# The second latent pass by pairs of items on two halves of TensorE's rows, the fourth attention's small banks rearranged, and weight rounding moved beside the tile attention

## The chip, the cores and the metric

One core of one Trainium2 chip runs the whole program in one launch. The metric is the device time of one execution in microseconds (us). The kernel before took 1465.81 us, the median of three runs (1461.55 to 1468.51).

## The reference, cut to what matters

The program is four layers over an activation `x` of 32 items by 128 rows by 128 columns in float32; each layer adds an attention and a feed-forward block to `x`. What the change touches is the routed block of layer 1, the ternary weights of layer 2, and the latent attention of layer 3:

```python
# layer 1, ffn: 63 rows of each batch picked, attention over them (16 heads), then gelu MLP, scattered back
# layer 2, ffn: weight_quant(w) = clip(round(w * scale), -1, 1) / scale, scale = 1 / mean(|w|)
# layer 3, ffn, attention half (N_HEADS 16, HEAD_DIM 8, KV_LATENT 64):
q = (x @ Wq.T).reshape(b, t, N_HEADS, HEAD_DIM)
latent = layernorm(x @ Wdkv.T, ln_g, ln_b)          # 64 wide
k = (latent @ Wuk.T).reshape(...); v = (latent @ Wuv.T).reshape(...)
q = apply_rope(q); k = apply_rope(k)
scores = jnp.where(causal, einsum('bhqd,bhkd->bhqk', q, k) / sqrt(HEAD_DIM), -inf)
out = einsum('bhqk,bhkd->bhqd', softmax(scores), v) @ Wo.T
```

In words: for every one of the 32 items, a 128 x 64 latent is normalised over its 64 columns, scaled by `ln_g` and shifted by `ln_b`, and multiplied with a 64 x 384 weight (key, key with halves turned for the rotation, value).

## The kernel before, in words

`x_all` holds the 32 items in SBUF for the whole run. The program is a list of stages (`phases`); all five engines meet at a barrier after each (`phase_end`, L971). Inside a stage every engine walks a software pipeline written with `steps` or `whole_steps`: at step t the stage function with lag n works on item t - n. What an engine waits for is a counting semaphore.

**The latent stage** (`latent_*`, from L1612) has two passes. The first turns x, multiplies it with `w_h1` (320 columns), rotates the queries and keeps the raw latents in `lat_raw`. Then VectorE works out mean and scale of all 32 latents at once. The second pass, over 32 items, is for each item:

- ScalarE `scale` (L1704) writes the normalised latent, 128 rows by 64 columns, to `o_sb`; two slots.
- TensorE `turn_latent` (L1737) transposes it into bank 4 or 5 of PSUM.
- ScalarE `take_turned` (L1711) applies `ln_g` and `ln_b` per partition and writes `oT`, 64 partitions by 128; two slots.
- TensorE `keys` (L1743) multiplies it with `w_h2` (64 x 384) into bank 6 or 7. A float32 product is two MATMUL instructions in the trace.
- VectorE `key` (L1661, L1662) multiplies the two 128-column halves with the rotation table into `probs`; GpSimd `key` (L1679) adds them into `kv_all`; ScalarE `take_v` (L1716) copies the value.

**The attentions** L0 to L4 share four functions. One step of `attention_tensor` is: `halves(.., 0)` (half of the raw scores of item t-2 and of the final scores of item t-4, L671, L696, L703, L713), `turns` (all small transposes and products), `mask_whole` (L722), `halves(.., 1)`, `weighted` (L860, item t-5), `mask_strips`. `turns` has a first part (transposes of o, q and k into bank 6, L800, L807, L808) and a last part (the product of oT with the output weight, L783, the transposed maxima, L776, and the picking of p times v, L827, in bank 7). `LOW` names the attentions whose last part comes first: there the turned maxima lie in bank 6, the output product in bank 7, the last part runs ahead of the first, VectorE takes o and adds the product to the stream ahead of taking qT, kT and oT, and `weighted` waits for the addition three items back in place of the copied maxima. Before, `LOW` holds L0, L2 and L3; L4, the causal latent attention with 16 heads over 32 items, is not in it.

**The rounding** of layer 2's weights (`expand_aside`) runs on GpSimd in the stage that expands the routed rows (`expand_*`), after the clearing of `v_wide`. The stage before it is the attention L1 over four tiles, in which GpSimd has little to do.

Of the kernel before, what the change touches and what calls it, by code (L numbers as in the profile page):

```python
# [11 lines left out]
ALU = mybir.AluOpType  # L12
# [3 lines left out]
B, S, D = 32, 128, 128  # L16
# [8 lines left out]
RING = 4  # L25
# [98 lines left out]
def build(nc, t_in, out):  # L124
    with ExitStack() as ctx_:
# [9 lines left out]
        def after(name, n=0):  # L135

            return sem(name), n + begun.get(name, 0)

        def sb(name, shape, dt=F32):
            return ctx_.enter_context(nc.sbuf_tensor(name, shape, dt))  # L140
# [130 lines left out]

        TURN_LAG = {True: 8, False: 6}

        LOW = ("L0", "L2") + ("L3",)

        def turned_max(L):

# [668 lines left out]
        causal = sb("causal", [128, 4, 128], BF16)  # L946
        rope = sb("rope", [128, 4, 128])
        w_h1 = sb("w_h1", [128, 320])
        w_h2 = sb("w_h2", [64, 384])
        w_o3 = sb("w_o3", [128, 128])  # L950
        gate_w = sb("gate_w", [128, N_EXP3])
        gate_b = sb("gate_b", [128, N_EXP3])
# [659 lines left out]
        lat_raw = ctx_all[:, 0:8, :].rearrange("p a b -> p (a b)").rearrange("p (b n) -> p b n", b=B)  # L1612
        lat_stat = ctx_all[:, 8, 0:6 * B].rearrange("p (b n) -> p b n", b=B)
        lat_scale, lat_shift = ctx_all[:, 9, 0:B], ctx_all[:, 9, B:2 * B]
        turned_halves = probs[:, 0, 0:1024].rearrange("p (k n) -> p k n", k=RING)

        def latent_vector(dve):
            V = nc.vector
            inv_both = inv_all[:, 0:B]
            V.scalar_tensor_tensor(shift_all[:], mean_all[:], -1.0, inv_ln[:], ALU.mult, ALU.mult  # L1620
                                   ).then_inc(sem("la_shift"), 1)

            def query(b, k):
                dve.wait_ge(*after("used", b + 1))
                wait_reuse(dve, after("la_q"), b, RING)
                src, own = ps[:, 2 + k, :], inv_both[:, b:b + 1]
                half = turned_halves[:, k, :]
                V.scalar_tensor_tensor(half[:, 0:128], src[:, 0:128], own, rope[:, 0, :], ALU.mult, ALU.mult)
                V.scalar_tensor_tensor(half[:, 128:256], src[:, 128:256], own, rope[:, 1, :], ALU.mult, ALU.mult)  # L1629
                V.bn_stats(lat_stat[:, b, :], src[:, 256:320]).then_inc(sem("la_halves"), 1)  # L1630
            steps(dve, B, [(3, query)])


            dve.wait_ge(sem("la_halves"), B)
            c = moments_taken["v"] = moments_taken.get("v", 0) + 1
            q = Seq(dve, sem("vector_step"), moments_taken)
            part, var, root, twice, apart = (moment[:, i, 0:B] for i in range(5))
            st = lat_stat
            q.count(V.tensor_tensor(apart, st[:, :, 1], st[:, :, 4], ALU.subtract))
            q.count(V.tensor_tensor(part, st[:, :, 2], st[:, :, 5], ALU.add))  # L1640
            q(V.tensor_tensor(twice, st[:, :, 1], st[:, :, 4], ALU.add))
            q.count(V.scalar_tensor_tensor(apart, apart, 0.25, apart, ALU.mult, ALU.mult))
            q(V.tensor_tensor(var, inv_both, inv_both, ALU.mult))
            q(V.scalar_tensor_tensor(part, part, 1.0 / LATENT, apart, ALU.mult, ALU.add))
            q(V.tensor_tensor(var, var, part, ALU.mult))
            q(V.tensor_scalar(var, var, 1e-5, None, ALU.add))
            dve.sem_inc(sem("variance"), 1)
            dve.wait_ge(sem("deviation"), c)
            q(V.reciprocal(apart, root))
            q(V.scalar_tensor_tensor(part, apart, -0.5, apart, ALU.mult, ALU.mult))  # L1650
            q(V.tensor_tensor(part, part, var, ALU.mult))
            q(V.scalar_tensor_tensor(apart, part, 1.5, apart, ALU.add, ALU.mult))
            q(V.tensor_tensor(lat_scale, apart, inv_both, ALU.mult))
            q(V.scalar_tensor_tensor(lat_shift, twice, -0.5, lat_scale, ALU.mult, ALU.mult))
            dve.sem_inc(sem("la_scaled"), 1)

            def key(b, k):
                dve.wait_ge(sem("la_kv"), b + 1)
                wait_reuse(dve, after("la_k"), b, RING)
                half, src = turned_halves[:, k, :], ps[:, 6 + k % 2, :]  # L1660
                V.tensor_tensor(half[:, 0:128], src[:, 0:128], rope[:, 2, :], ALU.mult)  # L1661
                V.tensor_tensor(half[:, 128:256], src[:, 128:256], rope[:, 3, :], ALU.mult  # L1662
                                ).then_inc(sem("la_key_halves"), 1)
            dve.wait_ge(sem("la_q"), B)
            steps(dve, B, [(3, key)])

        def latent_gpsimd(pool):
            pads_gpsimd(pool, 16)
# [4 lines left out]
                nc.gpsimd.tensor_tensor(q_all[:, b, :], half[:, 0:128], half[:, 128:256],  # L1673
                                        ALU.add).then_inc(sem("la_q"), 1)

            def key(b, k):
                pool.wait_ge(sem("la_key_halves"), b + 1)
                half = turned_halves[:, k, :]
                nc.gpsimd.tensor_tensor(kv_all[:, b, 0:128], half[:, 0:128], half[:, 128:256],  # L1679
                                        ALU.add).then_inc(sem("la_k"), 1)  # L1680
            steps(pool, B, [(4, query)])
            steps(pool, B, [(4, key)])

        def latent_scalar(act):
            nc.scalar.activation(w_h1[:], w_h1[:], ACT.Copy, scale=col("norm1")).then_inc(sem("la_weights"), 1)
# [13 lines left out]
            act.wait_ge(sem("la_scaled"), 1)  # L1699
            act.wait_ge(sem("la_raw"), B)  # L1700

            def scale(b, k):
                wait_reuse(act, after("la_latent_turned"), b, 2)
                nc.scalar.activation(o_sb[:, k % 2, 0:LATENT], lat_raw[:, b, :], ACT.Identity,  # L1704
                                     bias=lat_shift[:, b:b + 1], scale=lat_scale[:, b:b + 1]
                                     ).then_inc(sem("la_latent"), 1)

            def take_turned(b, k):
                act.wait_ge(sem("la_latent_turned"), b + 1)
                wait_reuse(act, after("la_kv"), b, 2)  # L1710
                nc.scalar.activation(oT[0:LATENT, k % 2, :], ps[0:LATENT, 4 + k % 2, 0:128], ACT.Identity,  # L1711
                                     bias=col("ln_b", LATENT), scale=col("ln_g", LATENT)).then_inc(sem("la_latentT"), 1)

            def take_v(b, k):
                act.wait_ge(sem("la_key_halves"), b + 1)
                nc.scalar.activation(kv_all[:, b, 128:256], ps[:, 6 + k % 2, 256:384],  # L1716
                                     ACT.Copy).then_inc(sem("la_v"), 1)
            steps(act, B, [(0, scale), (1, take_turned), (3, take_v)])

        def latent_tensor(pe):  # L1720
            pe.wait_ge(sem("la_weights"), 1)
# [9 lines left out]
            steps(pe, B, [(1, turn_x(pe)), (2, queries)])  # L1731
            pe.wait_ge(sem("la_raw"), B)

            def turn_latent(b, k):
                pe.wait_ge(sem("la_latent"), b + 1)
                wait_reuse(pe, after("la_latentT"), b, 2)
                nc.tensor.transpose(ps[0:LATENT, 4 + k % 2, 0:128], o_sb[:, k % 2, 0:LATENT],  # L1737
                                    ident[:]).then_inc(sem("la_latent_turned"), 1)

            def keys(b, k):  # L1740
                pe.wait_ge(sem("la_latentT"), b + 1)
                wait_reuse(pe, after("la_v"), b, 2)
                nc.tensor.matmul(ps[:, 6 + k % 2, 0:384], oT[0:LATENT, k % 2, :], w_h2[:], start=True,  # L1743
                                 stop=True).then_inc(sem("la_kv"), 1)
            steps(pe, B, [(1, turn_latent), (2, keys)])

# [132 lines left out]
        def expert_tensor(pe):  # L1881
# [39 lines left out]
            def group(i, k):  # L1921
# [64 lines left out]
            (w_tgt[:, 0:128], t_in["W_tgtT"]), (w_tgt[:, 128:256], t_in["W_outT"][0:128, :]),  # L1986
            (w_out2[:], t_in["W_outT"][128:256, :]),
            (w_h1[:, 0:128], t_in["WqT"]), (w_h1[:, 128:256], t_in["WqT_turned"]), (w_h1[:, 256:320], t_in["WdkvT"]),
            (w_h2[:, 0:128], t_in["WukT"]), (w_h2[:, 128:256], t_in["WukT_turned"]), (w_h2[:, 256:384], t_in["WuvT"]),
            (w_o3[:], t_in["WoT"]), (gate_w[:], t_in["gateT"]), (gate_b[:], t_in["gate_b"].partition_broadcast(128)),  # L1990
            (b1_col[:], t_in["b1T"]), (b2_col[:], t_in["b2T"]),
            (bias_cols[:, 0:1], t_in["b_in"].rearrange("(c p) -> p c", p=128)),
# [4 lines left out]
            (col("L2_b"), t_in["L2_b"].partition_broadcast(128)),  # L1997
            (col("router_b"), t_in["router_b"].partition_broadcast(128)),
            (rw_row[:], t_in["router_w"].rearrange("d one -> (one d)").partition_broadcast(128)),
        ] + [(col(n, t_in[n].shape[0]), t_in[n].rearrange("(s one) -> s one", one=1))  # L2000
             for n in ("g_res", "ln1", "ln2", "norm1", "norm2", "ln_g", "ln_b")]

# [117 lines left out]

        def expand_aside(pool):
            q = Seq(pool, sem("aside_seq"), moments_taken)
            V = nc.gpsimd
            pads_gpsimd(pool, 8)
            for w, i in ((w1_nat, 0), (w2_nat, 1)):
                q(V.tensor_scalar(w, w, inv_w[:, i:i + 1], MAGIC, ALU.mult, ALU.add))
                q(V.tensor_scalar(w, w, MAGIC, -1.0, ALU.subtract, ALU.max))
# [38 lines left out]
        def row_counts(**more):  # L2168
# [16 lines left out]
            dict(vector=gather_vector, scalar=gather_scalar, tensor=gather_tensor),  # L2185
            dict(vector=lambda e: attention_vector(e, "L1", TILES, 16, False, True),
                 counts=attention_counts("L1", TILES, 16, True),
                 gpsimd=lambda e: attention_gpsimd(e, "L1", TILES, 16, False),
                 scalar=lambda e: attention_scalar(e, "L1", TILES, 16, False, True),
                 tensor=lambda e: attention_tensor(e, "L1", TILES, 16, 3, tile_mask, w_o1[:])),  # L2190
            dict(vector=expand_vector, scalar=expand_scalar, tensor=expand_tensor, gpsimd=expand_aside),
            dict(vector=lambda e: attention_vector(e, "L2", B, 8, True, False),
                 counts=attention_counts("L2", B, 8, False),
                 gpsimd=lambda e: attention_gpsimd(e, "L2", B, 8, True),
# [149 lines left out]
```

## Time and profile before

| what | value |
|---|---|
| median of three runs | 1465.81 us |
| the profiled execution, whole | 1465.44 us |
| its span | 1463.7 us |
| TensorE's mean granted clock | 0.911 of full speed |
| TensorE busy | 1306.9 us, 89% of the span |
| latent stage, second pass | 923.6 to 987.0 us |
| attention L4 | 987.1 to 1191.6 us |

A time in a row is counted from the start of the span. PE is TensorE's MATMUL, PEld its weight load, DVE is VectorE, ACT ScalarE, POOL GpSimd; PEq, ACTq and so on are their sequencers. The column PEclk is the clock granted to TensorE, 1.00 being 2.4 GHz and 0.50 being 1.2 GHz. A shape such as 64*128 behind a matmul is the rows and columns of the array that it uses.

### The profile page before, as it was taken

What the parts mean: (1) busy time and instruction counts of PE and PEld (TensorE: products, weight loads), DVE (VectorE), ACT (ScalarE), POOL (GpSimd) and SP (SyncE); (2) the same over time, 40 slices, a digit from 0 to 9 for tenths busy, and PEclk for the clock granted to TensorE, in tenths of its full rate; (3) what the DMA queues carried; (4) which work ended last, traced back from release to release, by engine and by line L of the source; (5) the groups of instructions that cost most, each with busy time, mean ns of one, the idle gap of its engine ahead of it and who ended that gap; (6) DMA issues with size and microseconds to landing.
All of it is one profiled execution on the core that took longest, in us unless ns stands there. A gap on an engine that the chain in (4) does not pass through costs nothing. (4 is left out here: it accounts for less than half of the span.)

```text
span 1463.7 us, 37014 instructions
## 1 busy us (share of the span) xinstructions
PE 1306.9 (89%) x13899; PEld 861.5 (59%) x13899; DVE 932.4 (64%) x2810; ACT 605.9 (41%) x1375; POOL 277.2 (19%) x782
## 2 busy tenths in 40 slices
PE   3999988839759979998999997899999969999998
PEld 2888876635447754444657885337888844444443
DVE  4677749975367858996336886325777744454554
ACT  2788845641326642222443556542444421111111
POOL 0122211310313320000002223222454520000000
PEclk9999998958869989997998998656999979999999
DMA  9400000000000000000000000001000000000000
GB/s 288 121 3 3 3 2 2 2 1 1 2 1 2 3 2 1 1 1 1 1 1 2 3 3 1 1 0 59 3 3 3 3 2 0 15 8 7 7 7 15
DMA packets 26390, 21.31 MB, mean 15 GB/s; under 512 B 5936, under 2 KB 22512, under 8 KB 26224
## 3 DMA queue, kind: packets, MB, share of 16 engines
q1 hardware_dynamic: 25216, 18.87, 4.6%
q8 instruction: 112, 1.84, 0.5%
q14 instruction: 54, 0.44, 0.1%
q10 hardware_dynamic: 1008, 0.16, 0.1%
HBM read 16.93 MB, written 2.10 MB: 13 GB/s over the span
## 5 line engine op out<-in xcount | busy, mean ns | idle before, releaser
L703 PE MATMUL ps<-kT,qTm 32*128 32x128 f32 x3200 | 250.9, 291 | 1.2 <-issue 0.6
L671 PE MATMUL ps<-qTm,kT 32*128 32x512 f32 (+1 forms) x1024 | 249.1, 550 | 1.8 <-ACT probs L574 1.4
L703 PEld LDWEIGHTS ps<-kT,qTm 32*128 32x128 f32 x3200 | 226.1, 202 | 6.9 <-issue 4.2
L1933 PE MATMUL ps<-kv_all,ctx_all 128*128 128x512 f32 x256 | 134.1, 605 | 5.8 <-DVE kv_all L1846 5.8
L1870 ACT ACTIVATE kv_all<-ps,b_col 128x512 f32<-128x512 f32 x64 | 44.0, 687 | 216.5 <-PE ps L1911 216.5
L1911 PE MATMUL ps<-q_all,ctx_all 128*128 128x512 f32 x256 | 132.4, 600 | 0.0
L380 DVE TENSOR_REDUCE neg_max<-ps 128x8 f32<-128x1024 f32 x72 | 87.7, 1219 | 67.6 <-PE ps L703 67.3
L574 ACT ACTIVATE probs<-ps 128x1024 f32<-128x1024 f32 x72 | 73.8, 1024 | 119.7 <-PE ps L713 119.7
L860 PE MATMUL ps<-probs,v_wide 128*32 128x128 f32 x3200 | 115.2, 277 | 8.5 <-DVE o_sb L429 3.7
L1846 DVE TENSOR_SCALAR kv_all<-ps,b_col 128x512 f32<-128x512 f32 x64 | 48.0, 750 | 116.4 <-PE ps L1911 116.4
L671 PEld LDWEIGHTS ps<-qTm,kT 32*128 32x128 f32 x1024 | 85.2, 189 | 47.9 <-issue 38.8
L499 POOL CAST nm<-neg_max 128x16 bf16<-128x16 f32 (+1 forms) x132 | 27.0, 204 | 426.2 <-DVE neg_max L367 158.2
L375 DVE TENSOR_REDUCE neg_max<-ps 128x4 f32<-128x512 f32 x128 | 82.1, 683 | 34.2 <-PE ps L703 34.1
L394 DVE TENSOR_TENSOR qTm<-ps,hmask 128x512 f32<-128x512 f32 (+1 forms) x132 | 73.4, 556 | 38.4 <-ACT nmT L552 19.7
L570 ACT ACTIVATE probs<-ps,bias_col 128x512 f32<-128x512 f32 x128 | 81.1, 684 | 36.2 <-PE ps L713 36.2
L713 PE MATMUL ps<-nmT,sel_max 32*128 32x128 bf16 x1600 | 95.6, 218 | 0.0
L860 PEld LDWEIGHTS ps<-probs,v_wide 128*32 128x32 f32 x3200 | 80.7, 109 | 24.3 <-issue 13.9
L1529 PE MATMUL ps<-tap_w,xqT 128*128 128x512 f32 x192 | 93.6, 624 | 0.0
L1911 PEld LDWEIGHTS ps<-q_all,ctx_all 128*128 128x128 f32 x256 | 49.1, 192 | 61.3 <-issue 61.3
L564 ACT ACTIVATE probs<-ps,bias_col 128x1024 f32<-128x1024 f32 x64 | 71.4, 1115 | 32.1 <-PE ps L713 32.1
L827 PE MATMUL ps<-pv_pick,pv 128*128 128x72 f32 (+1 forms) x528 | 82.6, 279 | 1.0 <-ACT pv L580 0.9
L580 ACT ACTIVATE pv<-ps 128x256 f32<-128x256 f32 x132 | 50.7, 384 | 72.1 <-PE ps L860 69.6
(379 smaller groups left out, 2703.8 us busy)
## 6 DMA issues: line engine op xcount, KB each, us to landing
ctx_all<-in_ctx SPq DMA_DIRECT2D x4, 1024.0 KB, 10.5
x_all<-in_x SPq DMA_DIRECT2D x4, 512.0 KB, 7.1
out<-x_all SPq DMA_DIRECT2D x8, 256.0 KB, 2.3
ctx_all<-in_W1T SPq DMA_DIRECT2D x1, 1024.0 KB, 5.5
tap_w<-in_conv_wT SPq DMA_DIRECT2D x1, 768.0 KB, 6.9
w_l<-in_w SPq DMA_DIRECT2D x2, 256.0 KB, 3.7
above<-in_c_above SPq DMA_DIRECT2D x1, 256.0 KB, 3.4
rope<-in_c_rope SPq DMA_DIRECT2D x1, 256.0 KB, 2.7
```

The source lines that it names most:

```text
L375: nc.vector.tensor_reduce(neg_max[:, k, per * g:per * g + per], ps[:, raw_bank(L, b, g), 0:N].rearrange("p (h k) -> p h k", h=per), AX.X, ...
L380: nc.vector.tensor_reduce(neg_max[:, k, H2 * u:H2 * u + H2].rearrange("p (a h) -> p a h", a=2), ps[:, 4 * u:4 * u + 2, 0:N].rearrange("p a ...
L570: nc.scalar.activation(probs[:, k % 2, N * g:N * (g + 1)], ps[:, final_bank(L, b, g), 0:N], ACT.Exp, bias=bias).then_inc(sem("probs_ready" ...
L574: nc.scalar.activation(probs[:, k % 2, 2 * N * u:2 * N * (u + 1)].rearrange("p (a n) -> p a n", a=2), ps[:, 2:4, 0:N], ACT.Exp, bias=bias) ...
L671: nc.tensor.matmul(ps[:, bank, at:at + N], kT[rows_of(g), k, :], qTm[rows_of(g), k, 0:N], start=True, stop=False, skip_group_check=True)
L703: last = nc.tensor.matmul(dst, qTm[rows_of(g), k, 128 * i:128 * i + 128], kT[rows_of(g), k, :], start=False, stop=True, skip_group_check=True)
L713: last = nc.tensor.matmul(dst, sel_max[rows_of(g), i, :], nmT[rows_of(g), k, :], start=False, stop=True, skip_group_check=True)
L827: last = nc.tensor.matmul(ps[:, 7, 256 + W * half:256 + W * half + W], pv[:, k % 2, 128 * half:128 * half + 128], pv_pick[:, 0 if heads == ...
L860: last = nc.tensor.matmul(ps[32 * j:32 * j + 32, 7, 128 * half:128 * half + 128], v_tile(k % 2, heads, 4 * half + j, i), probs[:, k % 2, 1 ...
L1529: last = nc.tensor.matmul(dst, xqT[:, k % 2, tap:tap + 128], tap_w[:, tap, :], start=False, stop=tap == 2)
L1911: nc.tensor.matmul(ps[:, c % 2, :], w_up[:, c, :], xm_T[:, k, :], start=True, stop=True).then_inc(sem("mo_hidden"), 1)
L1933: nc.tensor.matmul(ps[:, 4 + e % 2, :], w_down[:, c, :], hid[:, c % 4, :], start=c % 4 == 0, stop=c % 4 == 3).then_inc(sem("mo_down"), 1)
```

## The change

Three things. First, the second latent pass works on 16 pairs of items. The two latents of a pair stand side by side in `o_sb` (128 columns), one transpose turns both, so that item 2p lies on partitions 0 to 63 and item 2p+1 on 64 to 127; `w_h2`, `ln_g` and `ln_b` are loaded a second time on partitions 64 to 127; the two products of a pair use rows 0 to 63 and 64 to 127 of TensorE and two banks; three pairs of banks take turns. VectorE rotates a pair with one instruction, GpSimd adds a pair with one, ScalarE scales with two, and takes the turned latents and the values with one each. Second, L4 joins `LOW`. Third, GpSimd rounds the weights at the end of its part in L1 (`round_weights`), and only clears `v_wide` in the expand stage.

```diff
-        LOW = ("L0", "L2") + ("L3",)
+        LOW = ("L0", "L2") + ("L3", "L4")
-        w_h2 = sb("w_h2", [64, 384])
+        w_h2 = sb("w_h2", [128, 384])
+        pair_halves = probs[:, 0, :].rearrange("p (k i n) -> p k i n", k=RING, i=2)
+        PAIRS = B // 2
+        def pair_banks(p):
+            at = 2 + 2 * (p % 3)
+            return ps[:, at:at + 2, :]
# VectorE
-                V.tensor_tensor(half[:, 0:128], src[:, 0:128], rope[:, 2, :], ALU.mult)
-                V.tensor_tensor(half[:, 128:256], src[:, 128:256], rope[:, 3, :], ALU.mult
+                wide = rope[:, 2:4, :].rearrange("p r n -> p (r n)").unsqueeze(1).broadcast_to([128, 2, 256])
+                V.tensor_tensor(pair_halves[:, k, :, :], pair_banks(p)[:, :, 0:256], wide, ALU.mult
# GpSimd
+                nc.gpsimd.tensor_tensor(kv_all[:, 2 * p:2 * p + 2, 0:128], half[:, :, 0:128], half[:, :, 128:256],
# ScalarE
+            def scale(p, k):
+                wait_reuse(act, after("la_latent_turned"), p, 2)
+                for b in (2 * p, 2 * p + 1):
+                    at = LATENT * (b % 2)
+                    nc.scalar.activation(o_sb[:, k % 2, at:at + LATENT], lat_raw[:, b, :], ACT.Identity,
+                                         bias=lat_shift[:, b:b + 1], scale=lat_scale[:, b:b + 1]
+            def take_turned(p, k):
+                act.wait_ge(sem("la_latent_turned"), p + 1)
+                wait_reuse(act, after("la_kv"), p, 2, 2)
+                nc.scalar.activation(oT[:, k % 2, :], ps[:, k % 2, 0:128], ACT.Identity,
+            def take_v(p, k):
+                act.wait_ge(sem("la_key_halves"), p + 1)
+                nc.scalar.activation(kv_all[:, 2 * p:2 * p + 2, 128:256], pair_banks(p)[:, :, 256:384],
+            steps(act, PAIRS, [(0, scale), (1, take_turned), (3, take_v)])
# TensorE
+            def turn_latents(p, k):
+                pe.wait_ge(sem("la_latent"), 2 * p + 2)
+                wait_reuse(pe, after("la_latentT"), p, 2)
+                nc.tensor.transpose(ps[:, k % 2, 0:128], o_sb[:, k % 2, :], ident[:])
+            def keys(p, k):
+                pe.wait_ge(sem("la_latentT"), p + 1)
+                wait_reuse(pe, after("la_v"), p, 3)
+                for i in range(2):
+                    rows = slice(LATENT * i, LATENT * i + LATENT)
+                    nc.tensor.matmul(pair_banks(p)[:, i, 0:384], oT[rows, k % 2, :], w_h2[rows, :], start=True,
+                                     stop=True).then_inc(sem("la_kv"), 1)
+            steps(pe, PAIRS, [(1, turn_latents), (2, keys)])
# loads: 6 DMAs of w_h2 in place of 3, and 2 more for ln_g, ln_b on partitions 64 to 127
# rounding
-        def expand_aside(pool):
+        def round_weights(pool):
-            pads_gpsimd(pool, 8)
-                 gpsimd=lambda e: attention_gpsimd(e, "L1", TILES, 16, False),
+                 gpsimd=lambda e: (attention_gpsimd(e, "L1", TILES, 16, False), round_weights(e)),
-            dict(vector=expand_vector, scalar=expand_scalar, tensor=expand_tensor, gpsimd=expand_aside),
+            dict(vector=expand_vector, scalar=expand_scalar, tensor=expand_tensor, gpsimd=lambda e: pads_gpsimd(e, 8)),
```

## Rows read from the trace of the kernel before

**Rows 1.** The page's first part: busy time, share of the span, instructions.
```profile
PE 1306.9 (89%) x13899; PEld 861.5 (59%) x13899; DVE 932.4 (64%) x2810; ACT 605.9 (41%) x1375; POOL 277.2 (19%) x782
```
**Rows 2.** Busy time by stretch (length, each engine, PEclk, DMA share, GB/s).
```profile
899.00:902.00 3.00, 3.00 (x15) 1.95 (x14) 2.61 (x13) 2.62 (x12) 1.82 (x4) 0.98 0.00 0
903.00:917.00 14.00, 14.00 (x65) 9.21 (x63) 14.00 (x65) 14.00 (x65) 9.69 (x22) 1.00 0.01 3
917.00:924.00 7.00, 2.17 (x9) 1.03 (x7) 5.86 (x28) 3.69 (x17) 2.49 (x6) 0.93 0.00 0
927.00:984.00 57.00, 57.00 (x90) 18.92 (x90) 14.57 (x60) 27.73 (x88) 13.61 (x30) 0.50 0.00 1
987.00:1012.00 25.00, 23.69 (x233) 16.92 (x237) 12.47 (x17) 5.05 (x8) 4.37 (x11) 0.51 0.27 85
1041.00:1098.00 57.00, 55.47 (x1136) 45.67 (x1134) 42.48 (x90) 27.00 (x40) 28.11 (x50) 1.00 0.01 3
```
**Rows 3.** The chain that ended last, in order of time: start, us, what.
```profile
927.16 1.58 PE ps L1743 x2
928.74 0.35 PE ps L1737
```
**Rows 4.** Instructions in order of time, second pass: ScalarE (start, us, what, [idle before]).
```profile
923.64 0.77 ACT L1704 ACTIVATE o_sb<-ctx_all 128x64 f32<-128x64 f32 x2 [1.61 <-DVEq L1655]
...
946.47 0.45 ACT L1711 ACTIVATE oT<-ps,cols 64x128 f32<-64x128 f32 x1 [0.98 <-PE ps L1737]
946.82 0.26 ACT L1716 ACTIVATE kv_all<-ps 128x128 f32<-128x128 f32 x1
946.98 0.43 ACT L1704 ACTIVATE o_sb<-ctx_all 128x64 f32<-128x64 f32 x1
```
**Rows 5.** The same view, end of the second pass and start of L4.
```profile
986.50 0.45 POOL L1679 TENSOR_TENSOR kv_all<-probs 128x128 f32<-128x128 f32 x1 [0.83 <-DVE probs L1662]
...
987.07 0.47 PE L807 MATMUL ps<-ident,q_all 128*128 128x128 f32 x1 [1.18 <-POOLq L971]
```
**Rows 6.** Single lines: op, count, duration ns min/median/max, first and last start, forms.
```profile
L394 DVE TENSOR_TENSOR qTm<-ps,hmask x132: 405/678/693, 23.2 to 1165.1; 128x512 f32<-128x512 f32 x68, 128x256 f32<-128x256 f32 x64
L580 ACT ACTIVATE pv<-ps x132: 377/384/386, 48.1 to 1186.9; 128x256 f32<-128x256 f32 x132
```
**Rows 7.** L1's final scores: the single line, then in order of time.
```profile
L675 PE MATMUL ps<-qTm,kT x32: 587/640/692, 351.5 to 380.3; 32*128 32x512 f32 x32
...
375.83 1.13 PE L675 MATMUL ps<-qTm,kT 32*128 32x512 f32 x4
```
**Rows 8.** Instructions in order of time, one step of L4.
```profile
1099.86 0.70 PE L671 MATMUL ps<-qTm,kT 32*128 32x512 f32 x2
...
1101.24 1.23 DVE L380 TENSOR_REDUCE neg_max<-ps 128x8 f32<-128x1024 f32 x1 [1.34 <-PE ps L703]
...
1102.38 0.68 DVE L394 TENSOR_TENSOR qTm<-ps,hmask 128x512 f32<-128x512 f32 x1
...
1102.51 0.28 ACT L552 ACTIVATE nmT<-ps 128x128 bf16<-128x128 bf16 x1 [0.16 <-PE ps L827]
...
1103.38 0.24 DVE L423 RECIPROCAL inv_den<-ps 128x16 f32<-128x16 f32 x1
...
1104.17 0.29 DVE L264 BATCH_NORM_STATS2 stats_all<-ctx_all 128x6 f32<-128x128 f32 x1
...
1105.55 0.70 PE L671 MATMUL ps<-qTm,kT 32*128 32x512 f32 x2
```
**Rows 9.** Instructions in order of time, the expand stage's GpSimd and one VectorE.
```profile
390.52 1.19 POOL L2140 MEMSET v_wide<- 128x1312 f32 x1 [15.94 <-SPq L971]
...
392.03 0.70 POOL L2128 TENSOR_SCALAR k_pad<-k_pad,inv_w 128x512 f32<-128x512 f32 x1
...
392.90 0.54 DVE L240 TENSOR_TENSOR moment<-moment 128x4 f32<-128x4 f32 x1
...
401.31 3.97 POOL L2133 TENSOR_TENSOR tap_w<-k_pad,tap_w 128x512 f32<-128x512 f32 x3
```

More of the change, by code:

```diff
@@ L1655, in latent_vector, with key @@
             dve.sem_inc(sem("la_scaled"), 1)
[L1657 to L1660, printed above, removed]
-                V.tensor_tensor(half[:, 0:128], src[:, 0:128], rope[:, 2, :], ALU.mult)
-                V.tensor_tensor(half[:, 128:256], src[:, 128:256], rope[:, 3, :], ALU.mult
+            def key(p, k):
+                dve.wait_ge(sem("la_kv"), 2 * p + 2)
+                wait_reuse(dve, after("la_k"), p, RING)
+                wide = rope[:, 2:4, :].rearrange("p r n -> p (r n)").unsqueeze(1).broadcast_to([128, 2, 256])
+                V.tensor_tensor(pair_halves[:, k, :, :], pair_banks(p)[:, :, 0:256], wide, ALU.mult
                                 ).then_inc(sem("la_key_halves"), 1)
             dve.wait_ge(sem("la_q"), B)
-            steps(dve, B, [(3, key)])
+            steps(dve, PAIRS, [(3, key)])
         def latent_gpsimd(pool):
@@ L1674, in query, with key @@
                                         ALU.add).then_inc(sem("la_q"), 1)
[L1676 to L1679, printed above, removed]
+            def key(p, k):
+                pool.wait_ge(sem("la_key_halves"), p + 1)
+                half = pair_halves[:, k, :, :]
+                nc.gpsimd.tensor_tensor(kv_all[:, 2 * p:2 * p + 2, 0:128], half[:, :, 0:128], half[:, :, 128:256],
                                         ALU.add).then_inc(sem("la_k"), 1)
             steps(pool, B, [(4, query)])
-            steps(pool, B, [(4, key)])
+            steps(pool, PAIRS, [(4, key)])
         def latent_scalar(act):
@@ L1700, in latent_scalar @@
             act.wait_ge(sem("la_raw"), B)
[L1702 to L1716, printed above, removed]
+            def scale(p, k):
[4 more added lines that the diff above has]
+                                         bias=lat_shift[:, b:b + 1], scale=lat_scale[:, b:b + 1]
+                                         ).then_inc(sem("la_latent"), 1)
+            def take_turned(p, k):
+                act.wait_ge(sem("la_latent_turned"), p + 1)
+                wait_reuse(act, after("la_kv"), p, 2, 2)
+                nc.scalar.activation(oT[:, k % 2, :], ps[:, k % 2, 0:128], ACT.Identity,
+                                     bias=col("ln_b"), scale=col("ln_g")).then_inc(sem("la_latentT"), 1)
+            def take_v(p, k):
+                act.wait_ge(sem("la_key_halves"), p + 1)
+                nc.scalar.activation(kv_all[:, 2 * p:2 * p + 2, 128:256], pair_banks(p)[:, :, 256:384],
                                      ACT.Copy).then_inc(sem("la_v"), 1)
-            steps(act, B, [(0, scale), (1, take_turned), (3, take_v)])
+            steps(act, PAIRS, [(0, scale), (1, take_turned), (3, take_v)])
         def latent_tensor(pe):
@@ L1732, in latent_tensor @@
             pe.wait_ge(sem("la_raw"), B)
[L1734 to L1745, printed above, removed]
+            def turn_latents(p, k):
+                pe.wait_ge(sem("la_latent"), 2 * p + 2)
+                wait_reuse(pe, after("la_latentT"), p, 2)
+                nc.tensor.transpose(ps[:, k % 2, 0:128], o_sb[:, k % 2, :], ident[:]).then_inc(sem("la_latent_turned"), 1)
+            def keys(p, k):
[6 more added lines that the diff above has]
+            steps(pe, PAIRS, [(1, turn_latents), (2, keys)])
         GROUPS = B // 4
@@ L1988, in build @@
             (w_h1[:, 0:128], t_in["WqT"]), (w_h1[:, 128:256], t_in["WqT_turned"]), (w_h1[:, 256:320], t_in["WdkvT"]),
-            (w_h2[:, 0:128], t_in["WukT"]), (w_h2[:, 128:256], t_in["WukT_turned"]), (w_h2[:, 256:384], t_in["WuvT"]),
             (w_o3[:], t_in["WoT"]), (gate_w[:], t_in["gateT"]), (gate_b[:], t_in["gate_b"].partition_broadcast(128)),
@@ L1999, in build @@
             (rw_row[:], t_in["router_w"].rearrange("d one -> (one d)").partition_broadcast(128)),
+        ] + [(w_h2[64 * i:64 * i + 64, 128 * c:128 * c + 128], t_in[w])
+             for i in range(2) for c, w in enumerate(("WukT", "WukT_turned", "WuvT"))
+        ] + [(col(n)[64:128, :], t_in[n].rearrange("(s one) -> s one", one=1)) for n in ("ln_g", "ln_b")
         ] + [(col(n, t_in[n].shape[0]), t_in[n].rearrange("(s one) -> s one", one=1))
```

## The prediction

> **What bounds the kernel now.** I read the page's first part, then busy time by stretch, then the chain of waits, then single steps in order of time. TensorE is busy for 89% of the span [rows 1], so the question for each part of the change is whether it shortens TensorE's own work where that is the chain.
>
> In the second latent pass it is. From 927 to 984 us TensorE is busy for 57.00 of 57.00 us at a granted clock of 0.50 (1.2 GHz), while VectorE has 14.57, ScalarE 27.73 and GpSimd 13.61 us of work [rows 2]. The chain is nothing but TensorE: 1.58 us for the key product's two instructions, 0.35 us for the transpose, so 1.93 us an item [rows 3]. The stretches around show that the clock is no property of the stage: it was 1.00 in the first pass (products on 128*128), fell in the gap of 917 to 924 us, in which TensorE did 2.17 us, and stayed low [rows 2]. The instructions that ran at 0.50 use 64 of the 128 rows, or 64 of the 128 columns.
>
> In L4 the middle stretch has TensorE busy for 55.47 of 57.00 us at 1.00, VectorE 42.48 [rows 2]. There it is the engine that counts, and an edit that only reorders it can win nothing but waits.
>
> **Part one, the pass by pairs.** Per pair the change removes one transpose, and puts the two key products on different rows.
>
> Do the two products run at once? No row shows it for 64 rows; the nearest is L1's final score: products on two groups of 32 rows, 512 columns. One instruction takes 587 to 692 ns, yet all four take 1.13 us [rows 7]: that is two after each other, not four. The instructions are the same kind (float32, own banks), so I take full overlap. Bounds for the four key instructions of a pair, from 1.58 us for two [rows 3]: 1.58 (both at once) and 3.16 (one after another). I take 1.58.
>
> The Trainium skill (TensorEngine Tiling (Array Packing), Key Properties) says that changing the tiling mode, not just the tile, drains TensorE. By that rule the drain between the 128-row transpose and the 64-row products stays, but comes 16 times and not 32; no row here prices it alone. It is inside the 0.35 and 1.58 us, and the sum goes by those.
>
> The transpose now loads 128 columns and not 64. The nearest full transpose at the low clock took 0.47 us [rows 5]; I add 0.05 to the 0.35 (bounds 0 and 0.12). So a pair costs 0.40 + 1.58 = 1.98 us at 1.2 GHz, against 3.86 before. Over the pass: from the scaling's start at 923.64 to GpSimd's end at 986.95 it took 63.3 us [rows 4, 5]. After: the first product starts 2.0 us in (two scalings, a transpose, a copy, one scaling more than now), then 16 x 1.98 less the transpose that the last step lacks = 31.3, and a tail: VectorE on 512 columns 0.68 [rows 6], GpSimd on 256, and hand-overs, 1.7 together. That is 35.0, a gain of 28.3 us if the clock stays at 0.50.
>
> The others have room beside 1.98 us. ScalarE: two scalings at 0.34 spacing, the turned latents at 0.35, the values at 0.16 [rows 4] plus 0.12 for the doubled width (0.38 for 256 columns [rows 6] against 0.26 for 128 [rows 4]): 1.32 us a pair. VectorE 0.68. GpSimd: 0.45 at 128 columns [rows 5], 3.97 for three of 512 [rows 9], so about 0.75.
>
> Will the clock stay low? In the pass now half of the array stands idle at any time; with both halves in use nothing does but the gaps. At 896 to 902 us work on the whole array brought the clock from 0.50 to 0.98 within a few us [rows 2]; in L4, on 32-row products, it took until 1012 [rows 2]. The pairs lie between. I give a rise during the pass 62 in 100, after some 10 us of it. Then TensorE would need half of 1.98, 1.0 us a pair, and ScalarE's 1.32 becomes the bound; I take 1.35. With about four pairs at 1.98 and twelve at 1.35: 12 x 0.63 = 7.6 less, of which a later rise takes some: 6.5. Part one gains 28.3 + 6.5 = 34.8 us.
>
> Behind the pass comes L4, whose first 25 us ran at 0.51 [rows 2]. Between the last key product and L4's first transpose then stand VectorE's 0.68, GpSimd's 0.75 and the barrier, about 3 us with TensorE idle; the gap at 917 to 924 dropped the clock. So I expect L4 to start low as before: 0, bounds -10 (it starts high) and +2 (the rise comes later by chance).
>
> **Part two, L4's small banks.** No instruction is added or removed. TensorE's step, 5.69 us from one L671 to the same one a step later (1099.86 to 1105.55 [rows 8]), stays. What moves is VectorE: qTm (1102.38 now) comes behind o, its addition and its statistics, which take 1103.38 to 1104.46 together, 1.1 us [rows 8]. It starts when L380 ends at 1102.47 at best: o, addition and statistics to 1103.5, qTm (0.68) to 1104.2, kT's copy of a quarter of its width to 1104.4. Its new wait, for the copy of the maxima (ends at 1102.79 [rows 8]), is met by then; behind it in VectorE's queue stand kT, oT and the second maxima, and for qTm the next step's scores wait, at 1105.55 [rows 8]. Slack 1.1 us: cost 0. `weighted` waits for an addition that ends 1 us earlier than o does now: it saves 0 to 0.1 us where that was tight. In the drain the product and L827 wait together for the copied p times v, and the addition three items back stands ahead of `weighted`: 0.2 to 0.5 us in each of three last steps. I take +0.5, bounds -2 and +3.
>
> **Part three, the rounding.** GpSimd is idle for 15.94 us before 390.52; the rounding lasts from 392.03 to 405.28, 13.3 us [rows 9]. It would run from 374.6 to 387.9 and end 2.6 us ahead of the stage. In the expand stage it hid behind TensorE's and ScalarE's chain, so its leaving saves only what it cost VectorE there: L240 took 0.54 us on 4 columns beside it [rows 9]; I take -0.4, bounds -0.54 and 0. In L1's tail it meets VectorE's chain of short instructions: 0 to +3. I take +0.2, net -0.2.
>
> The Trainium skill (SBUF — State Buffer, Who interferes with whom) says that a VectorE instruction with two SBUF inputs and a GpSimd instruction that reads SBUF exclude each other for a whole instruction. L240's row agrees. By that rule L448 (two SBUF inputs, three in a row) could be held in L1's tail; the +3 above covers it.
>
> **The loads.** Five more small DMAs on SP's queue, issued in L0, whose loads nobody on the chain awaits: 0.
>
> **Sum**, against the profiled execution's own 1465.44 us (its span 1463.7, and 0.4 under the median, so the same scale): 1465.4 - 34.8 + 0 + 0.5 - 0.2 = 1430.9; I say 1431.
>
> **The rivals.**
> - The clock stays at 0.50 through the pass. For it: 57 us at 0.50 with TensorE busy throughout [rows 2]; against: half of the array was unused. 1465.4 - 28.3 + 0.3 = 1437.4. Chance 25 in 100.
> - The clock is high and L4 starts high too: for it, the pass ends only 3 us before; against, the gap of 917 to 924. L4's first 25 us at 0.51 lose up to 10: 1421 to 1425. Chance 9.
> - The two products don't overlap (the change doesn't do what it says). For it: no row with 64 rows; against [rows 7]. 3.16 + 0.40 = 3.56 a pair, 57 us in all, gain 4.8 us: 1461. Chance 7.
> - Slower: L4's scores wait for qTm. Place: VectorE's new order, with its wait on ScalarE's copy of the maxima. If that copy falls behind ScalarE's second exponential, to where the next step begins now (1105.55 [rows 8]), qTm and kT end 0.9 and the hand-overs 0.3 later, and each of 32 steps grows by 1.2 us: +38. It decides from 1.05 us a step, where it eats part one; time then 1469 to 1475. Against it: the copy stands ahead of that exponential in ScalarE's order. Chance 4.
> The forecast itself has 53; 2 are left for what I don't see.
>
> **How the numbers follow.** The likeliest's own range is 1426 to 1436 (clock rise early or late, drain). The range 1422 to 1442 takes in the rival with the low clock and most of that with L4 high: about 85 in 100 on paper, which I count as 8 in 10. A measurement of this kernel tells about 0.5%, 7.3 us. Faster by more than that: the forecast, the low clock and the high L4, 53 + 25 + 9, and part of the unseen, 0.88; within: no overlap, 0.08; slower 0.04.
>
> **What would show it.** L1743's 64 instructions: starts in twos a few ns apart, a pair's step 1.98 us or, with a clock of 1.00 in the pass, near 1.35 and bounded by ScalarE (right); 3.5 us (no overlap). L4's step 5.69 us with no wait for L394 before L671 and L703 (right). GpSimd's rounding over by 388, and expand as long as before within 0.5 us. The prediction is wrong if the pass takes over 40 us, or if L4's middle step isn't 5.69.

## The result, and the profile after

The changed kernel takes 1422.44 us (median of 4, 1420.91 to 1427.89) against 1466.18 us on the same chip: ratio 0.9712, 95% interval 0.9676 to 0.9748. The medians differ by 43.7 us; 34.5 was said (1430.9 against 1465.4). The median stands 0.4 us inside the low end of the range of 1422 to 1442, and two of its four executions (1420.91 and 1421.04) lie below it. Its profiled execution took 1421.04 us, with a span of 1419.3 us and a mean granted clock of 0.929 (0.911 before).

The page's first part, after:

```profile
PE 1262.0 (89%) x13883; PEld 845.8 (60%) x13883; DVE 930.2 (66%) x2762; ACT 594.9 (42%) x1343; POOL 273.6 (19%) x766
```

The 16 fewer MATMULs are the transposes; TensorE's share is still 89% [rows 1]. Busy time by stretch, after (columns as in [rows 2]):

```profile
923.60:926.90 3.30, 2.86 (x8) 1.06 (x8) 0.19 (x1) 2.92 (x9) 0.00 (x0) 0.50 0.00 0
926.90:930.00 3.10, 3.10 (x10) 1.19 (x9) 1.19 (x2) 2.48 (x8) 1.33 (x2) 0.50 0.00 0
930.00:943.00 13.00, 12.79 (x55) 4.61 (x53) 7.27 (x11) 12.54 (x41) 7.36 (x11) 0.99 0.00 1
...
946.80:951.00 4.20, 2.62 (x38) 1.64 (x38) 1.56 (x3) 1.63 (x3) 0.57 (x1) 0.98 0.50 155
951.00:972.00 21.00, 20.35 (x215) 15.37 (x211) 11.27 (x15) 3.69 (x6) 4.99 (x11) 0.50 0.23 71
1000.00:1057.00 57.00, 56.79 (x1204) 46.04 (x1200) 45.03 (x95) 27.83 (x42) 28.14 (x51) 1.00 0.01 3
```

The second latent pass starts at the low clock, as before, but leaves it at 930.5, after three pairs; from there ScalarE is the full engine (12.54 of 13.00 us). L4 begins high (its first transpose is at 947.6) and the clock falls at 951. From the first scaling at 923.00 to GpSimd's end at 947.37 the pass took 24.4 us, where it took 63.3. In the middle of L4 57 us hold 1204 MATMULs where they held 1136 [rows 2]: L4's step became shorter, 5.45 us and not 5.69, which had been ruled out. The chain of waits in the pass (start, us, what):

```profile
924.96 1.60 PE ps L1753 x4
926.56 0.41 PE ps L1746
926.97 1.58 PE ps L1753 x4
928.55 0.41 PE ps L1746
...
930.76 0.84 PE ps L1753 x4
931.61 0.26 PE ps L1746
```

All four instructions of a pair take the 1.58 us that two took [rows 3], the transpose 0.41. L4, from its transposed maxima to the next step's scores, in order of time:

```profile
1053.54 0.22 PE L776 MATMUL ps<-identb,nm 128*128 128x128 bf16 x1
1053.69 0.41 PE L722 MATMUL ps<-causal,identb 32*32 32x512 bf16 x8
...
1054.02 0.29 DVE L429 TENSOR_TENSOR o_sb<-ps,inv_den 128x128 f32<-128x128 f32 x1
...
1054.75 0.67 DVE L394 TENSOR_TENSOR qTm<-ps,hmask 128x512 f32<-128x512 f32 x1
1054.99 0.39 PE L713 MATMUL ps<-nmT,sel_max 32*128 32x128 bf16 x8
1055.31 1.08 PE L860 MATMUL ps<-probs,v_wide 128*32 128x128 f32 x32
...
1056.65 0.70 PE L671 MATMUL ps<-qTm,kT 32*128 32x512 f32 x2
```

The weighted product (L860) starts 0.32 us after L713 does. The same place in the kernel before (in order of time, not among the rows ahead of the prediction):

```profile
1103.66 0.29 DVE L429 TENSOR_TENSOR o_sb<-ps,inv_den 128x128 f32<-128x128 f32 x1
1103.70 0.39 PE L713 MATMUL ps<-nmT,sel_max 32*128 32x128 bf16 x8
...
1104.20 0.32 PE L860 MATMUL ps<-probs,v_wide 128*32 128x128 f32 x4
```

There it is 0.50 us, and o ends at 1103.95, 0.25 before L860 starts: L860 waited for o. In L1's tail of the changed kernel (in order of time) VectorE is held:

```profile
384.62 3.96 POOL L2144 TENSOR_TENSOR tap_w<-k_pad,tap_w 128x512 f32<-128x512 f32 x3
385.42 3.31 DVE L448 SCALAR_TENSOR_TENSOR x_all<-q_all,place_keep,x_all 128x128 f32<-128x128 f32 x3
388.65 0.28 DVE L414 COPY oT<-ps 128x128 f32<-128x128 f32 x1
389.86 0.86 DVE L448 SCALAR_TENSOR_TENSOR x_all<-q_all,place_keep,x_all 128x128 f32<-128x128 f32 x3
```

### The profile page after: what moved, and what is told of

It reads as the page before. It is cut to its first block and busy times, and to the rows that moved or that the text cites. A ratio compares the mean times of both kernels' runs of the same rounds, so it can differ in the third digit from the quotient of the medians.

```text
span 1419.3 us, 36830 instructions
## 1 busy us (share of the span) xinstructions
PE 1262.0 (89%) x13883; PEld 845.8 (60%) x13883; DVE 930.2 (66%) x2762; ACT 594.9 (42%) x1343; POOL 273.6 (19%) x766
## 5 line engine op out<-in xcount | busy, mean ns | idle before, releaser
L671 PE MATMUL ps<-qTm,kT 32*128 32x512 f32 (+1 forms) x1024 | 251.5, 555 | 2.3 <-ACT probs L574 2.1
L860 PE MATMUL ps<-probs,v_wide 128*32 128x128 f32 x3200 | 116.9, 280 | 4.6 <-DVE o_sb L429 1.7
L671 PEld LDWEIGHTS ps<-qTm,kT 32*128 32x128 f32 x1024 | 85.7, 190 | 48.5 <-issue 39.4
L713 PE MATMUL ps<-nmT,sel_max 32*128 32x128 bf16 x1600 | 96.7, 219 | 0.0
L860 PEld LDWEIGHTS ps<-probs,v_wide 128*32 128x32 f32 x3200 | 81.1, 111 | 19.7 <-issue 6.5
```

The lines of the kernel that those rows point to most:

```text
L671: nc.tensor.matmul(ps[:, bank, at:at + N], kT[rows_of(g), k, :], qTm[rows_of(g), k, 0:N], start=True, stop=False, skip_group_check=True)
L713: last = nc.tensor.matmul(dst, sel_max[rows_of(g), i, :], nmT[rows_of(g), k, :], start=False, stop=True, skip_group_check=True)
L860: last = nc.tensor.matmul(ps[32 * j:32 * j + 32, 7, 128 * half:128 * half + 128], v_tile(k % 2, heads, 4 * half + j, i), probs[:, k % 2, 1 ...
```

## The experiments

**The parts alone.** Three kernels with one part each. A ratio is that of a run's time to the time of the kernel before, measured beside it on the same chip, with its 95% interval; the us behind it are that ratio's gain on the kernel before.

```diff
# a_only: the changed kernel with parts two and three taken back
# b_only: the kernel before with
+        LOW = ("L0", "L2") + ("L3", "L4")
# c_only: the kernel before with round_weights behind GpSimd's part in L1
```

> The kernel before with part one alone (the pass by pairs, and the loads that it needs). Theory after the traces: the pass gains 38.9 us (63.3 to 24.4), and L4's steady step is 5.69 us as before, so 1427 +- 2 us. The prediction's own term was a gain of 34.8: 1431. Rival: that part of the gain belongs to the change of L4 or of the rounding (the clock rises only in their company): the pass then takes over 30 us here.

Measured: 1427.35 us, ratio 0.9737 (0.9717 to 0.9756): 38.6 us. In its trace a pair again takes 1.99 us at first (1.58 and 0.41), then 1.1 and from the eighth on 1.27; the pass is 25.1 us long. The pass's gain is its own.

> The kernel before with L4 in LOW, and nothing else. Theory after the traces: L4's steady step falls from 5.69 to 5.45 us by this edit alone, some 27 steps, so 1459 to 1461 (5 to 6.5 us faster). The prediction's term: step 5.69, 1466. Rival: the shorter step comes from what part one leaves behind (places of the keys, the clock); the step then stays 5.69 here.

Measured: 1460.45 us, ratio 0.9959 (0.9943 to 0.9975): 6.0 us. L4's steps, one after the other:

```profile
1101.52 0.70 PE L671 MATMUL ps<-qTm,kT 32*128 32x512 f32 x2
...
1105.30 0.39 PE L713 MATMUL ps<-nmT,sel_max 32*128 32x128 bf16 x8
1105.62 1.08 PE L860 MATMUL ps<-probs,v_wide 128*32 128x128 f32 x32
...
1106.97 0.70 PE L671 MATMUL ps<-qTm,kT 32*128 32x512 f32 x2
```

5.45 us. From L4's first transpose of q to its last there are 171.0 us (177.2 before), while the drain behind it is 0.6 us longer, as forecast.

> The kernel before with the rounding moved into L1's stage, and nothing else. Theory after the traces: three L448 instructions of VectorE are held beside GpSimd's products of two SBUF inputs (3.3 us in place of 0.86), L1's tail grows by 1.5 to 2 us, the expand stage gains 0.4 to 1.0: 1466 to 1467. The prediction's term: 1465.2. Rival: L1's tail was later in the changed kernel for another reason; L448 x3 then stays near 0.9 us and the stage pair 85.5 us.

Measured: 1466.76 us, ratio 1.0003 (0.9988 to 1.0018): no change in time. The three L448 take 3.32 us, where the changed kernel has 3.31, and from the end of the last copy of v to the next stage's memset there are 17.5 us, where GpSimd's idle time shows 15.94 [rows 9]. The 1.6 us lost in L1's tail are seen in the trace; whether anything gives them back isn't shown. The parts add up to 38.6 + 6.0 - 0.4 = 44.2 us by their ratios, and all three together have 42.2 by theirs (36.9 to 47.5): nothing shows that one part needs another.

**Why L4's step is shorter.** VectorE's order alone:

```diff
-                if L in LOW:
+                if L in LOW or L == "L4":
                     at(6, take_o)
...
-                if L not in LOW:
+                if L not in LOW and L != "L4":
                     at(6, take_o)
```

> The kernel before, in L4 alone VectorE takes o ahead of qT, kT and oT; TensorE's order, the banks and all waits stay as before. Theory: of the 0.24 us a step, 0.185 was the wait of the weighted product (L860) for o, which ended 0.22 us before it started; so here L860 starts right behind L713 and the step is 5.50 us, 5 us in all: 1461. Rival 1: the wait is not for o but for ScalarE's nmT or pv, which this edit leaves: step 5.69. Rival 2: the gain is all in TensorE's own order (L783, L827 first): step 5.69 here and 5.45 in the kernel with L4 in LOW.

Measured: 1461.32 us, ratio 0.9953 (0.9939 to 0.9967). In order of time (its lines from L672 on are one further down):

```profile
1101.03 0.70 PE L672 MATMUL ps<-qTm,kT 32*128 32x512 f32 x2
...
1101.47 0.29 DVE L429 TENSOR_TENSOR o_sb<-ps,inv_den 128x128 f32<-128x128 f32 x1
...
1101.99 0.39 PE L714 MATMUL ps<-nmT,sel_max 32*128 32x128 bf16 x8
...
1102.31 1.08 PE L861 MATMUL ps<-probs,v_wide 128*32 128x128 f32 x32
```

L861 stands 0.32 us behind L714, and the L672 of the next step comes at 1106.53, so a step is 5.50 us. Rival 1 is refuted: ScalarE's copies were left as they were. By time this kernel and `b_only` can't be told apart (the intervals overlap); the split that follows is read from the steps of the traces. Of the 0.24 us, 0.19 was the wait for o, and moving one VectorE instruction removes it. The other 0.05 belongs to TensorE's order: from L783 to L722 there are 1.26 us with the picking product last and 1.20 with the transposed maxima last.

**What the two halves at once are worth.** In one kernel the second product waits for the first:

```diff
                 for i in range(2):
+                    if i:
+                        pe.wait_ge(sem("la_kv"), 2 * p + 1)
                     rows = slice(LATENT * i, LATENT * i + LATENT)
```

> The changed kernel, but the second key product of a pair waits for the end of the first: the same instructions on the same two row halves, not at once. Theory: being at once is what brings the gain, twice: it halves the product's 3.16 us, and with both halves of the array at work the clock rises. Then a pair takes 3.6 us here, the clock stays at 0.50 for most of the pass, the pass takes 58 to 60 us, and the whole 1456 to 1459. Rival 1: the clock rises all the same after some pairs (it asks only for TensorE being busy): some 1.95 us a pair from there, pass 35 to 40 us, 1433 to 1438. Rival 2: the gain was in fewer transposes and hand-overs: 1425.

Measured: 1457.97 us, ratio 0.9927 (0.9909 to 0.9945); the pass took 60.1 us. Busy time by stretch, then the chain:

```profile
927.00:980.00 53.00, 52.13 (x75) 16.74 (x74) 9.91 (x15) 18.14 (x52) 10.15 (x14) 0.50 0.00 0
```

```profile
928.62 1.59 PE ps L1755 x2
930.21 0.04 issue
930.25 1.64 PE ps L1755 x2
931.89 0.40 PE ps L1746
932.30 1.59 PE ps L1755 x2
```

3.68 us a pair at 0.50 throughout. The overlap brings both things: half the product's time, and the rising clock. The full 128*128 transpose, which is the same in both kernels, doesn't raise it by itself.

**Is the low clock the half array's, or the gap's?** The kernel before, with TensorE kept at work between the passes:

```diff
             pe.wait_ge(sem("la_raw"), B)
+            for _ in range(36):
+                nc.tensor.transpose(ps[:, 7, 384:512], ident[:], ident[:])
```

> The kernel before with 36 transposes of the identity (no use for the result) on TensorE between the two latent passes, where it sat idle for 6 us, so that the single-item pass starts with the clock high. Theory: products on half of the array don't hold the clock; it falls back to 0.50 within some us, the pass takes over 58 us, the whole 1462 to 1466. Rival: it was the gap alone that took the clock, and the pass by single items holds it: 1.0 to 1.35 us an item, pass 34 to 43 us, the whole 1436 to 1445; part one's gain was then mostly the clock's.

Measured: 1436.72 us in a single execution, so without an interval; the six of the kernel before beside it have a median of 1467.86 (1465.72 to 1469.45). Busy time by stretch, then the chain:

```profile
918.00:923.00 5.00, 4.18 (x37) 3.99 (x37) 3.43 (x17) 1.67 (x7) 0.88 (x2) 1.00 0.00 0
923.00:957.00 34.00, 33.71 (x96) 12.79 (x95) 15.00 (x62) 29.23 (x92) 13.65 (x30) 1.00 0.00 1
```

```profile
924.54 0.23 PE ps L1742
924.77 0.84 PE ps L1748 x2
```

My theory fell: the clock did not fall back. Single items on half of the array, 1.07 us each (0.84 and 0.23), hold the high clock for all of the pass, though 57 us of the same products never raised the low one [rows 2]. What took it was the gap ahead of them. So 36 instructions of no use alone bring 31 us. A pair of items costs 3.86 us as singles at 0.50, 1.98 as a pair at 0.50, 2.14 as singles at 1.00, and 1.27 as a pair at 1.00.

> The changed kernel with 36 transposes of the identity (no use for the result) on TensorE between its two latent passes, as the earlier run had them on the kernel before. Theory: the pass by pairs now starts high as well, its first three pairs take 1.1 to 1.3 us and not 1.98, the pass 22 us and not 24.4: 1420. So with the clock high in both, the pairs are worth 1436.7 less the other parts' 6 less 1420, 10 to 12 us, and not 38.9. Rival: the transposes delay the first pair or take ScalarE's time by their writes to the accumulators: 1422 or more.

Measured: 1421.56 us (1414.64 to 1425.27), ratio 0.9695 (0.9667 to 0.9723), not told apart from the changed kernel's 0.9712. The pass starts at 1.00 and its pairs take 1.1 to 1.27 us. What are the pairs worth where the clock is high anyway? By the passes themselves 14.0 us: 36.3 in the kernel before with the 36 transposes, 22.3 here, as 16 x (2.14 - 1.27) has it. By the whole times less the other parts' 5.6 us it is 1436.7 - 1421.6 - 5.6 = 9.5. The first number is the pass's; the second has in it one execution alone, a spread of 10.6 us among this kernel's six, and an L4 whose first five steps took 30.5 us here and 28.2 there.

**The start of L4.** 12 such transposes behind the last key product, 7 ahead of the first scores:

```diff
             steps(pe, PAIRS, [(1, turn_latents), (2, keys)])
+            keep_busy(0, 12)
# in attention_tensor's step
+                if L == "L4" and 2 in items and items[2][0] == 0:
+                    keep_busy(2, 7, 0)
```

> The changed kernel with 12 transposes of the identity behind the last key product and 7 ahead of L4's first scores, in time in which TensorE sat idle (2.4 and 0.8 us). In the changed kernel the clock was still high for L4's first 4 us and then low until 24 us later. Theory: those gaps take the clock; filled, L4 starts and stays high, its first five steps take 17 to 22 us and not 29.3, the whole 1412 to 1416. Rival: the first steps' small products don't hold the clock, which falls a few us later: 1420 to 1424.

Measured: 1418.71 us (1413.41 to 1423.49), ratio 0.9671 (0.963 to 0.9713); its four executions took 1413.41, 1414.27 (the profiled one), 1423.15 and 1423.49, with mean clocks of 0.933, 0.934, 0.926 and 0.924. Busy time by stretch:

```profile
947.00:953.00 6.00, 5.83 (x83) 4.40 (x83) 3.96 (x6) 1.13 (x2) 0.00 (x0) 1.00 0.75 255
953.00:960.00 7.00, 6.81 (x69) 4.93 (x67) 4.05 (x6) 0.63 (x2) 1.08 (x5) 0.56 0.31 87
960.00:970.00 10.00, 8.74 (x185) 6.56 (x182) 6.22 (x9) 4.57 (x8) 5.41 (x10) 0.97 0.01 2
```

The fall came later and was short in this execution. Two executions lie where the theory has them and two where the rival has them; the median between them describes neither. Where the clock fell in the two long ones no trace shows.

**The rounding.** Its first six instructions ahead of GpSimd's part in L1, the three products behind it:

```diff
-                 gpsimd=lambda e: (attention_gpsimd(e, "L1", TILES, 16, False), round_weights(e)),
+                 gpsimd=lambda e: (round_weights(e, False), attention_gpsimd(e, "L1", TILES, 16, False), round_weights(e, True)),
```

> The changed kernel with the first six rounding instructions ahead of GpSimd's part in L1, where it waits 11 us for the first maxima, and only the three products for the taps (4 us) behind it. Theory: the three L448 instructions of VectorE are no longer held for 3.3 us beside the products, L1's tail is 1.6 us shorter (16.2 us from the last copy of v to the next stage's memset, 17.8 in the changed kernel), the whole 1420.5 to 1421. Rival: L448 is held wherever GpSimd works, also at L1's start, and the gain is given back there: 1422.

Measured: 1422.64 us, ratio 0.9683 (0.9666 to 0.9701): by time not told apart. In order of time:

```profile
373.89 3.95 POOL L2145 TENSOR_TENSOR tap_w<-k_pad,tap_w 128x512 f32<-128x512 f32 x3
377.73 0.87 DVE L448 SCALAR_TENSOR_TENSOR x_all<-q_all,place_keep,x_all 128x128 f32<-128x128 f32 x3
383.97 0.86 DVE L448 SCALAR_TENSOR_TENSOR x_all<-q_all,place_keep,x_all 128x128 f32<-128x128 f32 x3
...
389.87 1.19 POOL L2152 MEMSET v_wide<- 128x1312 f32 x1 [12.03 <-SPq L971]
```

No L448 group in the tail is held, and the tail is 15.9 us again. One at L1's start is, beside the first rounding instructions, as the rival has it:

```profile
333.88 1.67 DVE L448 SCALAR_TENSOR_TENSOR x_all<-q_all,place_keep,x_all 128x128 f32<-128x128 f32 x3
```

The Trainium skill (SBUF — State Buffer, Who interferes with whom) says that a VectorE instruction with two SBUF inputs and a GpSimd one that reads SBUF exclude each other for a whole instruction. Beside the products the trace of the changed kernel agrees: the three L448 end 0.15 us behind one product each, 3.31 us in all against 0.86. Beside the other rounding instructions it agrees only in part: there three L448 took 1.04 us from 379.18, all inside one GpSimd instruction of 1.92 us (378.94 to 380.86; spans of GpSimd are rough in a profile).

**Together.** `best1` has the 36, the 12, the 7 and the early rounding.

> The changed kernel with all three edits: 36 transposes between the passes, 12 behind the last key product and 7 ahead of L4's first scores, and the first six rounding instructions at L1's start. Theory: the gains add: 2.2 (pass) + 6.2 (L4) + 1.6 (L1's tail) under 1422.4, so 1412 to 1413. Rival: where L4's clock falls is chance, and its part is 0 to 6: 1413 to 1419.

Measured: 1416.84 us, ratio 0.9666 (0.9643 to 0.9688). L4's clock fell at 953.4 and stayed low for 17 us. The gains didn't add, and the rival (1413 to 1419) held.

```diff
-                if L == "L4" and 2 in items and items[2][0] == 0:
+                if L == "L4" and 2 in items and items[2][0] <= 2:
                     keep_busy(2, 7, 0)
```

> As the last, with 7 transposes ahead of the first scores half in each of L4's first three items and not of one alone. In the run with 7 the clock still fell for 7 us (954 to 961), with products on 32 rows alone on TensorE. Theory: whole-array work among them keeps the clock: L4's first five steps take 18 to 20 us and not 23, the whole 1409 to 1411. Rival: the transposes lie on TensorE's path there (VectorE has only 0.3 us a step more to do), and what they take, twice 0.76 us a step, is what they give: 1413.

Measured: 1411.35 us, ratio 0.9632 (0.9609 to 0.9655). Busy time by stretch:

```profile
947.00:953.00 6.00, 6.00 (x83) 4.57 (x84) 4.04 (x6) 0.67 (x2) 0.20 (x1) 1.00 0.90 273
953.00:960.00 7.00, 6.64 (x112) 5.06 (x111) 5.09 (x7) 1.47 (x3) 1.79 (x5) 1.00 0.25 69
960.00:970.00 10.00, 8.74 (x190) 6.75 (x186) 6.57 (x10) 4.81 (x7) 5.39 (x11) 1.00 0.02 3
```

L4 runs at 1.00 from its first step, its first five steps take 21.9 us (29.3 in the changed kernel), and the interval lies below the changed kernel's. 18 to 20 had been expected for the five steps; what took the rest wasn't traced. `best3` fills the gaps at the starts of other stages as well.

> As the last, and the same filling wherever TensorE idles at the start of another stage: 26 transposes before L2, 40 before the ternary feed-forward, 30 before the cross attention, 19 before the first latent pass, 36 before the experts, 48 at the end of the expand stage, 9 and 18 ahead of the first scores of L2 and L3, and 7 in each of L1's first three items. In the last run's records the clock was low for 24, 13.6, 17, 17, 10 and 17 us from those starts (98 us). Theory: the gap at a stage's start takes the clock everywhere; most of these stretches go, and since TensorE bounds about half of the work in them, the whole is 15 to 35 us shorter: 1376 to 1396. Rival 1: the first steps' small products let the clock fall in the attentions whatever stands before: 1400 to 1408. Rival 2: the fillers overrun the gaps and delay the first items, 0.5 us a stage, with no clock gained: 1413.

Measured: 1408.72 us, ratio 0.9597 (0.9575 to 0.962); the mean clock rose from 0.939 to 0.950 only. My theory (1376 to 1396) fell: the intervals of the last two overlap. By those mean clocks the low time went from some 172 to some 141 us (an estimate), and the median is still only 2.6 us lower; what the fillers cost elsewhere wasn't traced. Behind L2's fillers the clock fell in its first steps:

```profile
424.00:428.00 4.00, 3.21 (x38) 2.20 (x36) 2.23 (x5) 0.66 (x2) 0.03 (x1) 1.00 0.02 4
428.00:434.00 6.00, 4.79 (x50) 3.68 (x54) 3.18 (x6) 1.31 (x4) 1.30 (x7) 0.65 0.01 1
434.00:440.00 6.00, 6.00 (x75) 4.56 (x70) 2.36 (x4) 2.64 (x5) 1.54 (x8) 0.50 0.01 3
```

That is what the first rival says, though the time lies just above its 1400 to 1408. It is still the fastest kernel here, some 14 us below the changed one.

## Why the prediction was right, and where it was not

Of the forecast gain the pass and its reason were right and its size was nearly right; L4's step was wrong, and the two misses together brought the time to the range's edge.

**The pass (34.8 said, 38.6 measured alone).** The mechanism was right to the hundredth at the low clock: 0.41 and 1.58 us where 0.40 and 1.58 were said. The mis-sized term is the clock's 6.5, which came to 10.3 (38.6 - 28.3): the rise came some 5 us after the first product, three pairs on, and not after some 10 us, and a pair then took 1.10 and later 1.27 us, with ScalarE full, and not 1.35. The reason for the rise, both halves in use, is shown (3.68 us a pair at 0.50 with the same instructions in turn). But "half of the array stands idle" as the reason for the old pass's low clock is only half of it: that work could not raise the clock, and would have held it.

**L4's start (0 said, -10 to +2).** "So I expect L4 to start low as before": it started high, at 0.98, and fell some 3 us in, at 951. First transpose to sixth took 29.3 us against 28.5, so the sum's 0 came out near, but by luck: the high start was taken back by a low stretch that lasted 27 us into L4, where it had lasted 25.

**L4's step (5.69 said to stay) is the step that failed,** by the prediction's own sign for it ("or if L4's middle step isn't 5.69"). "An edit that only reorders it can win nothing but waits" was right as a sentence, and the waits were not looked for in the right row. TensorE's 55.47 of 57.00 us [rows 2] left 0.15 us a step, which reads as nothing to win and is about that wait. `weighted` was said to gain 0 to 0.1 us "where that was tight"; it was tight by 0.19 us a step. In the kernel before L429's end and L860's start stand 0.25 us apart, and rows 8 skip both. With the 0.05 of TensorE's order that is 0.24 x 26, 6.2 us, less the drain's 0.6 that was said as +0.5. That the whole stayed in the range is luck: its low edge had been drawn for another case, L4 at a high clock (1421 to 1425), and the likeliest's own range of 1426 to 1436 was missed. The sum's two large errors went the same way: 3.8 us in the pass, and 6.5 in L4, where `b_only` gained 6.0 and a cost of 0.5 had been said.

**The rounding (-0.2 said, 0 to +3 for the tail).** The three held L448 were named and priced inside the +3, but the value taken was 0.2; the tail lost 1.6. In time it can't be told from no change. "L240's row agrees" was read too strongly: L240's 0.54 us end at 393.44, while the GpSimd instruction beside it ends at 394.74, and L1443, with two SBUF inputs too, took 0.69 us beside the same instruction and 0.69 in the changed kernel with GpSimd idle.

**The rivals.** The high L4 came for 3 us only. The no-overlap rival was priced 1.8 us too low: with 3.56 us a pair its own terms give 16 x 3.56 - 0.40 + 2.0 + 1.7 = 60.3 us for the pass, a gain of 3.0 and not 4.8, and with the two products in turn it took 60.1. No overlap, a low clock through the pass, and L4 waiting for qTm did not come: qTm and kT end at 1055.6, 1.0 us ahead of the next L671, the slack that was said.

## What to carry to other kernels

Look up what the clock was doing ahead of a stage that runs low at full TensorE load: where a gap took it, a few transposes of the identity in the gap can be worth nearly as much as a rewrite of the stage (31 us against 38.6 here), and the rewrite must be valued at the clock it will then have. Where one engine counts, subtract for each of its groups the end of the last input from the start: a wait of 0.2 us a step is 3% of the step, and hides in a busy share that reads as full. Work moved to an idle engine should be laid against what runs beside it and where its operands lie, not against that engine's idle time alone.

## What the runs showed of the hardware that I had not expected

- The granted clock has a memory. The same single-item products left it at 0.50 for 57 us when they met it low, and at 1.00 for 34 us when they met it high.
- Products on 64 rows, two at once, raised it from 0.50; the same in turn, with TensorE busy 52.13 of 53.00 us, did not. Which measure of TensorE's activity decides stays open.
- Whether the small products of L4's first steps hold the clock changes with what stands between them: with 7 transposes once it fell in both profiled executions (for 7 and for 17 us), with 7 in each of three items it did not, in `best2` and in `best3`. Why it fell so differently in the first two, and why the fillers did less for L2, wasn't settled.
